# Row maxima of an attention taken over key tiles instead of from separate scores, in a one-core decoder layer

## The chip, the cores and the metric

The kernel runs on one core of a Trainium2 chip. The metric is the time of one execution on the device in microseconds; lower is better. TensorE (PE) multiplies matrices from SBUF into PSUM, VectorE (DVE), ScalarE (ACT) and GpSimd (POOL) do the elementwise work, SyncE (SP) issues most of the DMAs. PSUM has eight banks of 512 f32 for each of 128 partitions.

## The reference

One decoder layer on x [8, 512, 512] (f32) with a context [8, 512, 1024] and a mask over 512 positions of each of 8 batches. Three parts, each followed by a residual and a layer norm: a self-attention whose softmax runs over the 8 entries of the first axis (16 heads of 32), a cross attention (8 heads of 64), and a feed forward (512 to 2048 to 512) with a quantised hidden layer. The change touches the cross attention only:

```python
src_trans = (src @ W_src.T + b_src) * mask[:, :, None]      # [8, 512, 1024]: keys, values
tgt_trans = (tgt @ W_tgt.T + b_tgt) * mask[:, :, None]      # [8, 512, 512]: queries
scores = einsum('bthd,bshd->bhts', q, k) / sqrt(64)
scores = where(mask[:, None, None, :] == 0, -inf, scores)
attn = softmax(scores, axis=-1)
tgt_update = einsum('bhts,bshd->bthd', attn, v)
out = concatenate([tgt, tgt_update], axis=2) @ W_out.T + b_out
```

## The kernel before

The program has two halves, phase_a and phase_b (L955). phase_a does the self-attention and projects the context, and leaves the normed rows, the keys (already turned) and the values in HBM scratch, each as a high and a low f16 part. phase_b, in which the change lies, goes over the 8 batches. Every f32 product is made of three f16 products, high x high, low x high and high x low (terms, L47).

For each batch phase_b makes queries (queries, L1215; queries_masked, queries_hi and queries_low split them), then for 8 heads the attention, then the output projection (output_x1 for the half that needs no attention, output_rest for the other), a layer norm, and the turn of the normed rows into x2T (x2_transposes). The feed forward of a batch runs one turn of the loop later: while the heads of batch b+1 are worked, feed_forward1 (16 tiles of 12 matmuls, 128x512 out, into b_ff) and feed_forward2 (4 tiles of 16) of batch b fill TensorE between the steps of a head. In the heads of batch 0 there is no such work; there weight_transposes(n), n from 0 to 15, takes its place: four transposes of a w1 tile and four of a w2 tile into the two b_ff banks. It waits until ScalarE has copied the w2 tile of job n-1 (w2_done) and until VectorE has made the low part of the w1 tile of job n-1 (w1_lo).

A head's attention needs, for each query, the negated maximum of its scores as a row added by the product, since the scores that are used lie with keys on partitions (b_st) and the exponential's bias is a column over keys:

- scores(b, h, half), L1227: two matmuls each, queries on partitions, keys (512) along the bank, into b_sx0 and b_sx1;
- maximum, L1569: VectorE adds the mask row mneg and takes the maximum over 512 keys, for each of four tiles of 128 queries, into mxb; then L1580 writes the negated column into mz;
- maximum_row, L1235: four matmuls turn the column into a row of b_mr, and ScalarE copies that row into row 64 of q2 (L1408);
- transposed_scores(b, h, half), L1242: for each of four tiles of 128 keys two matmuls into b_st0 or b_st1, k1 x q1 (high and low keys with high queries) and k2 x q2 (high keys with low queries, and the row of maxima);
- exponentials, exponentials_high on ScalarE, exponentials_low on VectorE: exp into f32, then a high and a low f16 part, two key tiles at a time (p_hi, p_lo: 128x1024);
- values, L1253: 48 matmuls of 65 or 64 columns into b_av; normalized on VectorE divides by the sum.

The order in each engine's queue is written out by hand in heads (TensorE L1312, ScalarE L1462, VectorE L1612), and waits are semaphore counts. The maxima of head h+1 are found while head h is worked: TensorE's order in head h is scores(h+1, first half), transposed_scores(h, first half), values(h-1), scores(h+1, second half), feed_forward1(2h+1), transposed_scores(h, second half), maximum_row(h+1), feed_forward1(2h+2). The first head's scores come in queries_and_first_scores (L1357), amid the last tile of queries, and VectorE's side of it is queries_and_first_maximum (L1634). PSUM: two banks b_st, two b_sx, two b_ff, b_av and b_mr; at a batch's end the same banks serve for queries (tq_b) and for the output projection (om_b).

## Time and profile before

| | us |
|---|---|
| median of 3 runs | 1929.81 |
| lowest, highest | 1927.22, 1932.05 |
| the profiled execution | 1929.76 |
| its span, first to last instruction | 1927.9 |

| engine | busy us | share of the span |
|---|---|---|
| TensorE, matmuls | 1829.5 | 95% |
| TensorE, weight loads | 1003.3 | 52% |
| VectorE | 1333.2 | 69% |
| ScalarE | 785.3 | 41% |
| GpSimd | 558.7 | 29% |

phase_b takes from about 820 us to the end. Its batch 0 lies from about 835 to 935 us; each of the seven turns of the loop behind it takes about 129 us. In the rows L12 is line 12 of the kernel; PE is TensorE's matmuls, PEld its weight loads. A row's time is the start in us from the span's first instruction, and then the duration; matmuls overlap, so the distance between starts is what one costs in a row of them, and the duration is from its start to its last result. An idle time in brackets names what ended it.

### The profile page before, as it was taken

The page shows a single profiled execution, that of the slowest core. Times are in us where ns is not written, and L with a number is a line of the kernel's source. Part 1 is how long each engine was busy: PE and PEld are TensorE (multiplying, and loading weights), DVE is VectorE, ACT ScalarE, POOL GpSimd, SP SyncE. Part 2 cuts the span into 40 slices and gives each one's busy share as a digit, 9 for nine tenths or more (in the row PEclk, how much of TensorE's full clock was granted, in tenths as well). Part 3 has the DMA queues.
Part 4 walks back from the last instruction along what each step waited for, and adds up shares of the span by engine and source line. Part 5 has one row for each costly group of instructions (what it writes and reads, how often), then busy time and mean ns, then how long its engine had stood idle before and what let it go on. Part 6 is the DMA issues. An engine that isn't in the chain of part 4 may idle for free. (4 is left out here: it accounts for less than half of the span.)

```text
span 1927.9 us, 33302 instructions
## 1 busy us (share of the span) xinstructions
PE 1829.5 (95%) x12476; PEld 1003.3 (52%) x12476; DVE 1333.2 (69%) x1676; ACT 785.3 (41%) x1208; POOL 558.7 (29%) x576
## 2 busy tenths in 40 slices
PE   7999999999999989878899999999999999999998
PEld 3665465546554646445455454455454554554543
DVE  2899998999899998667465554655655646556521
ACT  3423222222222222248365363562653635626522
POOL 3135964786368345400102002003011020030010
PEclk9999999999999999979999999999999999999999
DMA  8436355425633566574413406207135052071010
GB/s 212 124 79 151 78 152 143 116 77 151 150 94 99 125 172 137 150 167 157 99 39 61 122 1 116 66 1 138 44 51 131 1 111 72 1 133 27 12 33 22
DMA packets 322654, 183.97 MB, mean 95 GB/s; under 512 B 225584, under 2 KB 278832, under 8 KB 322511
## 3 DMA queue, kind: packets, MB, share of 16 engines
q1 hardware_dynamic: 316448, 178.37, 38.9%
q10 hardware_dynamic: 6062, 3.49, 0.8%
q8 instruction: 114, 1.87, 0.4%
q14 instruction: 30, 0.24, 0.0%
HBM read 94.75 MB, written 33.55 MB: 67 GB/s over the span
## 5 line engine op out<-in xcount | busy, mean ns | idle before, releaser
L1531 DVE TENSOR_TENSOR p_lo<-k,p_hi 128x1024 f16<-128x1024 f32 x128 | 156.8, 1225 | 194.4 <-ACT p_hi L1404 194.4
L1176 POOL TENSOR_TENSOR q<-q,x_hi 128x512 f16<-128x512 f32 x28 | 37.6, 1374 | 638.7 <-ACT x_hi L1457 638.7
L1576 DVE CUSTOM_DVE_ANT_0 junk<-b_sx,mneg 128x512 f16<-128x512 f32 x256 | 175.9, 687 | 32.6 <-issue 23.2
L1204 PE MATMUL b_ff<-x2T_hi,w1T_hi 128*128 128x512 f16 x512 | 194.7, 380 | 1.9 <-DVE x2T_lo L1531 1.9
L1204 PE MATMUL b_ff<-x2T_lo,w1T_hi 128*128 128x512 f16 x512 | 194.7, 380 | 0.0
L1204 PE MATMUL b_ff<-x2T_hi,w1T_lo 128*128 128x512 f16 x512 | 194.6, 380 | 0.0
L1436 ACT ACTIVATE k<-b_st,mbias 128x512 f32<-128x512 f32 x256 | 161.9, 685 | 14.0 <-PE b_st L1250 13.4
L577 PE MATMUL sm_b<-cT_hi,wsT_hi 128*128 128x256 f16 x512 | 141.8, 277 | 15.2 <-DMA cT_lo<-rows_lo 13.6
L784 DVE TENSOR_TENSOR prod<-q,k 128x4096 f32<-128x4096 f32 x32 | 142.2, 4443 | 17.5 <-ACT q L660 16.7
L1404 ACT ACTIVATE p_hi<-k 128x1024 f16<-128x1024 f32 x128 | 135.3, 1057 | 45.5 <-PE b_av L1265 43.1
L1428 ACT ACTIVATE hq<-b_ff,b 128x512 fp8e4<-128x512 f32 x128 | 88.0, 687 | 155.6 <-PE b_ff L1204 149.0
L543 PE MATMUL pj_b<-winT_hi,xT_hi 128*128 128x512 f16 x384 | 146.8, 382 | 0.9 <-DVE winT_lo L851 0.9
L543 PE MATMUL pj_b<-winT_lo,xT_hi 128*128 128x512 f16 x384 | 146.8, 382 | 0.0
L543 PE MATMUL pj_b<-winT_hi,xT_lo 128*128 128x512 f16 x384 | 146.5, 382 | 0.0
L824 DVE TENSOR_TENSOR prod<-pr,v 128x4096 f32<-128x4096 f32 x32 | 142.4, 4451 | 1.1
L577 PE MATMUL sm_b<-cT_hi,wsT_lo 128*128 128x256 f16 x512 | 141.7, 277 | 0.0
L577 PE MATMUL sm_b<-cT_lo,wsT_hi 128*128 128x256 f16 x512 | 141.7, 277 | 0.0
L789 DVE TENSOR_REDUCE pr<-prod 128x128 f32<-128x4096 f32 x32 | 141.1, 4410 | 0.1
L1413 ACT ACTIVATE q<-q,rstdb 128x512 f32<-128x512 f32 x64 | 52.2, 815 | 216.4 <-POOL rstdb L88 216.3
L440 POOL TENSOR_TENSOR rows_lo<-cn,rows_hi 128x512 f16<-128x512 f32 x64 | 117.0, 1835 | 61.0 <-ACT rows_hi L644 60.9
L1204 PE MATMUL b_ff<-w2T,hq 128*128 128x512 fp8e4 x512 | 112.9, 379 | 1.6 <-ACT hq L1428 1.0
L82 POOL TENSOR_TENSOR vsb<-mvb,consts 128x1 f32<-128x1 f32 x64 | 14.9, 233 | 337.6 <-DVE mvb L1546 337.6
(272 smaller groups left out, 4368.9 us busy)
## 6 DMA issues: line engine op xcount, KB each, us to landing
cn<-in_ctx_dram SPq DMA_DIRECT2D x64, 256.0 KB, 3.1
k<-kT_scratch SPq DMA_DIRECT2D x24, 512.0 KB, 7.7
x<-in_x_dram SPq DMA_DIRECT2D x32, 256.0 KB, 3.1
x_scratch<-x SPq DMA_DIRECT2D x32, 256.0 KB, 2.2
q<-x_scratch SPq DMA_DIRECT2D x8, 1024.0 KB, 5.6
q<-x_scratch SPq DMA_DIRECT2D x32, 256.0 KB, 2.9
out_dram<-q SPq DMA_DIRECT2D x32, 256.0 KB, 4.4
xn<-in_x_dram SPq DMA_DIRECT2D x24, 256.0 KB, 2.9
```

Of the source, the lines that this page charges most:

```text
L440: pool.tensor_tensor(lo[:, :], row_source(kind, i), hi[:, :], ALU.subtract).then_inc(s["row_lo"], 1)
L543: pe.matmul(out, a, c, start=(j == 0 and m == 0), stop=False)
L577: pe.matmul(dst, a, z, start=(j == 0 and m == 0), stop=False)
L784: dve.tensor_tensor(prod[:, :, :], q[:, t, :].unsqueeze(1).to_broadcast([P, T, E]), k[:, :, :], ALU.mult).then_inc(s["sc_prod"], 1)
L789: dve.tensor_reduce(pr[:, t].rearrange("p h s -> p s h"), prod[:, :, :].rearrange("p s (h d) -> p s h d", h=H1), AX.X, ALU.add).then_inc(s ...
L824: dve.tensor_tensor(by_head(prod), probs, by_head(v), ALU.mult).then_inc(s["av_prod"], 1)
L1204: mm = pe.matmul(out, a, c, start=(start and n == 0), stop=end)
L1404: act.activation(dst, src, ACT.Copy, scale=scale).then_inc(done, 1)
L1428: act.activation(hq[:, f, :], ff_b[f % 2][:, :], ACT.Relu, bias=b1[:, f:f + 1], scale=1.0 / WS, saturate=False).then_inc(s["relu"], 1)
L1436: act.activation(pf[:, st, :], st_b[st % 2][:, :], ACT.Exp, bias=mbias[:, st:st + 1], scale=D2 ** -0.5).then_inc(s["st_exp"], 1)
L1531: dve.tensor_tensor(dst, bank, hi, ALU.subtract).then_inc(out, 1)
L1576: dve.tensor_tensor_reduce(junk[:, :], sx_b[tt % 2][:, :], mneg[:, :], 1.0, NEG, ALU.add, ALU.max, mx[:, h % 2, tt:tt + 1]).then_inc(s["sx ...
```

## The change

The scores with queries on partitions, their two banks and the mask row mneg are gone. b_st has four banks. For each head first_scores makes k1 x q1 into the four banks and leaves the sums open. On VectorE tops adds a mask column (0 or -60000) to each of the four banks in turn and keeps the larger of it and what top holds, element by element, so that top (128x512, f16) holds for each of 128 key positions and each query the maximum over the four key tiles. turned_tops turns top into b_mr by four matmuls with minus the identity, one tensor_reduce (negated_maxima) takes the minimum over 128 columns into mz, and maximum_row is as before. second_scores then adds k2 x q2 to the four open banks. The maximum is that of the first products alone; the softmax doesn't depend on the exact number subtracted.

The order is new on three engines. feed_forward1 can be issued in parts (i to j of its 12 matmuls); the first scores of head h+1 lie between parts of feed_forward1(2h+2), each behind the exponential that empties its bank; the turn lies before feed_forward1(2h+3), and maximum_row in it. For batch 0 a part that doesn't begin at 0 is nothing, and a part that does is the whole weight_transposes. The diff, cut to its core:

```diff
-    st_b = [bank(f"b_st{i}") for i in range(2)]
-    sx_b = [bank(f"b_sx{i}") for i in range(2)]
+    st_b = [bank(f"b_st{i}") for i in range(4)]
...
-    tq_b, om_b = [*st_b, mr_b, av_b], [*sx_b, *ff_b]
+    tq_b, om_b = [*st_b[0:2], mr_b, av_b], [*st_b[2:4], *ff_b]
...
-            def scores(b, h, half):
...
+            def first_scores(b, h, st):
+                if h:
+                    pe.wait_ge(s["st_exp"], 32 * b + 4 * (h - 1) + st + 1)
+                pe.matmul(st_b[st][:, :], k1[:, h, st * P:(st + 1) * P], q1[:, h, :], start=True,
+                          stop=True).then_inc(s["first_filled"], 1)
+
+            def turned_tops(b, h):
+                pe.wait_ge(s["topped"], 32 * b + 4 * h + 4)
+                for tt in range(4):
+                    mm = pe.matmul(mr_b[:, tt * P:(tt + 1) * P], top[:, tt * P:(tt + 1) * P], minus16[:, :],
+                                   start=True, stop=True)
+                mm.then_inc(s["mr_filled"], 1)
...
-            def transposed_scores(b, h, half):
...
+            def second_scores(b, h):
+                pe.wait_ge(s["mr_copied"], 8 * b + h + 1)
+                for st in range(4):
+                    pe.matmul(st_b[st][:, :], k2[:, h, st * P:(st + 1) * P], q2[:, h, :], start=False,
+                              stop=True, skip_group_check=True).then_inc(s["st_filled"], 1)
...
-            def feed_forward1(b, f):
+            def feed_forward1(b, f, i=0, j=12):
                 if b is None:
-                    return weight_transposes(f)
+                    return weight_transposes(f) if i == 0 else None
...
             def output_x1(ff):
+                if ff is None:
+                    pe.wait_ge(s["st_exp"], 32)
...
             def heads(b, ff):        # TensorE
                 feed_forward1(ff, 0)
                 pe.wait_ge(s["q_masked"], 4 * b + 4)
+                turned_tops(b, 0)
+                feed_forward1(ff, 1, 0, 6)
                 maximum_row(b, 0)
+                feed_forward1(ff, 1, 6, 12)
                 for h in range(H2):
+                    second_scores(b, h)
+                    if h + 1 == H2:
+                        values(b, h - 1)
+                        continue
+                    f = 2 * h + 2
...
-                    if h + 1 < H2:
-                        scores(b, h + 1, 0)
-                    transposed_scores(b, h, 0)
+                    feed_forward1(ff, f, 0, 2)
+                    first_scores(b, h + 1, 0)
+                    feed_forward1(ff, f, 2, 4)
+                    first_scores(b, h + 1, 1)
                     if h == 1:
                         pe.wait_ge(s["v_ld"], 80 * (b + 1))
                     if h:
                         values(b, h - 1)
-                    if h + 1 < H2:
-                        scores(b, h + 1, 1)
-                    feed_forward1(ff, 2 * h + 1)
-                    transposed_scores(b, h, 1)
-                    if h + 1 < H2:
-                        maximum_row(b, h + 1)
-                        feed_forward1(ff, 2 * h + 2)
+                    first_scores(b, h + 1, 2)
+                    feed_forward1(ff, f, 4, 6)
+                    first_scores(b, h + 1, 3)
+                    feed_forward1(ff, f, 6, 12)
+                    turned_tops(b, h + 1)
+                    feed_forward1(ff, f + 1, 0, 5)
+                    maximum_row(b, h + 1)
+                    feed_forward1(ff, f + 1, 5, 12)
...
             def queries_and_first_scores(b, ff):
-                scores(b, 0, 0)
+                first_scores(b, 0, 0)
+                first_scores(b, 0, 1)
                 queries(b, 3, slice(8, None))
-                scores(b, 0, 1)
+                first_scores(b, 0, 2)
+                first_scores(b, 0, 3)
...
             def heads(b, ff, rows=True):        # ScalarE
                 for h in range(H2):
+                    if h + 1 == H2:
+                        relu(ff, 2 * h + 1)
                     exponentials(b, h, 0)
+                    if h + 1 < H2:
+                        relu(ff, 2 * h + 1)
+                    exponentials(b, h, 1)
                     exponentials_high(b, h, 0)
-                    relu(ff, 2 * h + 1)
-                    exponentials(b, h, 1)
-                    if h + 1 < H2:
-                        maximum_row(b, h + 1)
                     exponentials_high(b, h, 1)
                     if h + 1 < H2:
                         relu(ff, 2 * h + 2)
+                        maximum_row(b, h + 1)
...
-            def maximum(b, h, half):
...
+            def tops(b, h, half):
+                for st in (2 * half, 2 * half + 1):
+                    n = 32 * b + 4 * h + st
+                    dve.wait_ge(s["first_filled"], n + 1)
+                    if st == 0:
+                        dve.tensor_scalar(top[:, :], st_b[0][:, :], mleast[:, 0:1], None, ALU.add).then_inc(
+                            s["topped"], 1)
+                    else:
+                        dve.wait_ge(s["topped"], n)
+                        stand_alone(dve, alone["dve"])
+                        dve.scalar_tensor_tensor(out=top[:, :], in0=st_b[st][:, :], scalar=mleast[:, st:st + 1],
+                                                 in1=top[:, :], op0=ALU.add, op1=ALU.max).then_inc(s["topped"], 1)
+
+            def negated_maxima(b, h):
+                dve.wait_ge(s["mr_filled"], 16 * b + 2 * h + 1)
+                dve.tensor_reduce(mz[:, 4 * (h % 2):4 * (h % 2) + 4, D2],
+                                  mr_b[:, :].rearrange("p (t c) -> p t c", t=4), AX.X, ALU.min).then_inc(s["negm"], 1)
...
             def heads(b, ff):        # VectorE
                 w1_low(ff, 0)
+                negated_maxima(b, 0)
+                w1_low(ff, 1)
                 for h in range(H2):
                     if h + 1 < H2:
-                        maximum(b, h + 1, 0)
+                        tops(b, h + 1, 0)
+                        tops(b, h + 1, 1)
+                    exponentials_low(b, h, 0)
+                    if h + 1 < H2:
+                        w1_low(ff, 2 * h + 2)
+                        negated_maxima(b, h + 1)
                     if h:
                         normalized(b, h - 1)
-                    if h + 1 < H2:
-                        maximum(b, h + 1, 1)
-                    exponentials_low(b, h, 0)
-                    w1_low(ff, 2 * h + 1)
                     exponentials_low(b, h, 1)
                     if h + 1 < H2:
-                        w1_low(ff, 2 * h + 2)
+                        w1_low(ff, 2 * h + 3)
...
-                maximum(b, 0, 0)
                 queries_low(b, 2)
+                tops(b, 0, 0)
                 queries_masked(b, 3)
-                maximum(b, 0, 1)
                 queries_low(b, 3)
+                tops(b, 0, 1)
```

In batch 0, ScalarE's relu(None, f) is weights_high(f), two copies out of the b_ff banks, and w1_low is VectorE's low part of the same tile; for all other batches w1_low is nothing.

## Rows read from the trace of the kernel before

**Rows 1.** Stretches: busy us (x instructions) by engine, PEclk the granted clock, DMA.
```profile
851.00:856.00 5.00, 2.98 (x18) 1.28 (x15) 4.58 (x12) 2.88 (x5) 0.00 (x0) 0.90 0.24 59
861.00:866.00 5.00, 3.56 (x12) 2.04 (x13) 2.58 (x4) 2.21 (x3) 0.00 (x0) 0.58 0.80 209
876.00:916.00 40.00, 33.05 (x400) 22.25 (x398) 33.07 (x75) 35.27 (x55) 0.00 (x0) 1.00 0.35 109
1493.00:1622.00 129.00, 127.06 (x949) 65.02 (x948) 73.17 (x151) 66.72 (x97) 14.80 (x36) 1.00 0.31 67
```

**Rows 2.** Timeline, TensorE, heads of batch 5: start, us, engine, line.
```profile
1512.23 0.59 PE L1232 MATMUL b_sx<-k,q 128*128 128x512 f16 x2
...
1541.09 0.59 PE L1232 MATMUL b_sx<-k,q 128*128 128x512 f16 x2
...
1542.56 0.20 PE L1262 MATMUL b_av<-v_hi,p_hi 128*128 128x65 f16 x1
...
1544.02 0.59 PE L1232 MATMUL b_sx<-k,q 128*128 128x512 f16 x2
...
1547.04 0.38 PE L1249 MATMUL b_st<-q,k 128*128 128x512 f16 x1
...
1547.90 0.39 PE L1238 MATMUL b_mr<-ident,mz 128*65 128x128 f16 x4
1548.13 0.38 PE L1204 MATMUL b_ff<-x2T_hi,w1T_hi 128*128 128x512 f16 x1
```

**Rows 3.** Timeline, the same batch: handovers between the engines.
```profile
1550.89 1.23 DVE L1531 TENSOR_TENSOR p_lo<-k,p_hi 128x1024 f16<-128x1024 f32 x1 [3.20 <-ACT p_hi L1404]
...
1551.00 0.69 ACT L1428 ACTIVATE hq<-b_ff,b 128x512 fp8e4<-128x512 f32 x1
...
1552.18 0.20 PE L1262 MATMUL b_av<-v_hi,p_hi 128*128 128x65 f16 x1 [0.44 <-DVE p_lo L1531]
...
1557.34 7.07 PE L1204 MATMUL b_ff<-w2T,hq 128*128 128x512 fp8e4 x32
...
1564.44 0.69 DVE L1606 TENSOR_TENSOR f16o<-b_ff,b2q 128x512 f16<-128x512 f32 x1 [0.98 <-PE b_ff L1204]
```

**Rows 4.** VectorE: groups by line and form (busy us, mean ns), one timeline row.
```profile
L1576 DVE CUSTOM_DVE_ANT_0 junk<-b_sx,mneg 128x512 f16<-128x512 f32 x224 | 153.9, 687 | 26.5 <-issue 20.4 <-PE b_sx L1232 6.1
L1563 DVE SCALAR_TENSOR_TENSOR qf<-b_st,bt,mrow 128x512 f32<-128x512 f32 x14 | 10.5, 750 | 5.4 <-PE b_st L1204 4.9
...
L789 DVE TENSOR_REDUCE pr<-prod 128x128 f32<-128x4096 f32 x32 | 141.1, 4410 | 0.1
...
1596.91 0.18 DVE L1546 BATCH_NORM_AGGREGATE mvb<-statsb 128x2 f32<-128x6 f32 x1 [0.15 <-DVE statsb L1543]
```

**Rows 5.** Timeline, the start of batch 6's heads.
```profile
1607.25 1.28 DVE L1531 TENSOR_TENSOR x2T_lo<-b_ff,x2T_hi 128x512 f16<-128x512 f32 x2
...
1607.58 0.59 PE L1232 MATMUL b_sx<-k,q 128*128 128x512 f16 x2
...
1622.11 0.59 PE L1232 MATMUL b_sx<-k,q 128*128 128x512 f16 x2
```

**Rows 6.** Timeline, batch 0: heads 0, 2 and 7, ScalarE in head 6, output_x1.
```profile
854.51 0.39 PE L1249 MATMUL b_st<-q,k 128*128 128x512 f16 x1 [0.25 <-ACT q L1408]
...
875.29 0.38 PE L1249 MATMUL b_st<-q,k 128*128 128x512 f16 x1
...
905.61 0.59 ACT L1408 ACTIVATE q<-b_mr 1x512 f16<-1x512 f32 x1
906.23 1.06 ACT L1404 ACTIVATE p_hi<-k 128x1024 f16<-128x1024 f32 x1
...
908.28 1.27 ACT L1436 ACTIVATE k<-b_st,mbias 128x512 f32<-128x512 f32 x2
...
915.19 0.38 PE L1249 MATMUL b_st<-q,k 128*128 128x512 f16 x1
...
920.01 0.38 PE L1204 MATMUL b_sx<-wxT_hi,x1T_hi 128*128 128x512 f16 x1
```

58 lines of the change are left out of this document (18 added, 40 removed).

## The prediction

> **What bounds the kernel now.** I read the busy time by stage first, then TensorE's order of time in one head, then what VectorE and ScalarE hand to it. From batch 1 on TensorE is the bound: 127.06 of 129.00 us at a granted clock of 1.00, VectorE and ScalarE near half [rows 1]. A head takes (1541.09 - 1512.23) / 3 = 9.62 us [rows 2]. The 512-column matmuls start 3.02 / 14 = 0.216 us apart, the 48 of values() take 1.46, the four of maximum_row 0.23 (1547.90 to 1548.13) [rows 2]; 36 x 0.216 + 1.46 + 0.23 = 9.47 is work and 0.15 is waiting. A matmul ends 0.38 us after it starts [rows 2]. A wait that VectorE ends costs TensorE 0.06 (1552.12 to 1552.18), one that TensorE ends costs VectorE 0.03 (1564.41 to 1564.44) [rows 3]. In batch 0 the heads hold weight transposes in place of feed forward products; TensorE isn't full there, and VectorE and ScalarE set 7.98 us a head, (915.19 - 875.29) / 5 [rows 6].
>
> **What goes and what comes, in counts.** Each of 64 heads loses 4 of 36 matmuls (the scores with queries on partitions) and gains four of 128 columns. TensorE work per full head becomes 32 x 0.216 + 1.46 + 0.23 + 0.23 = 8.83, 0.64 less. If that were all, 56 heads would give 36 us. But the row of maxima now takes a longer way: four VectorE operations that hang on each other, a turn on TensorE, a reduction on VectorE, the old turn, the copy. And first_scores fill all four b_st banks, so each waits for an exponential of the head before.
>
> **New VectorE costs.** tops() is a scalar_tensor_tensor with a pointer scalar on a PSUM tile: its nearest row is L1563, 0.75 us; the removed reduction, 0.687, is the lower bound. Each waits for the one before with a stand_alone between, as BATCH_NORM_AGGREGATE does: 0.15; the lower bound is none [rows 4]. The first top has no second tensor; I put it at 0.75 too. tensor_reduce over 512: 1024 elements of p_lo take 1.23 and 512 of L1576 take 0.687 [rows 3, 4], so 1.06 ns an element and 0.14 fixed, 0.68; an eighth of the 4.41 for 4096 elements, 0.55, is the lower bound [rows 4]. The row shows 0.75 for 512 f32 elements from PSUM with a pointer scalar. The Trainium skill (VectorE: DVE Perf Modes, the section on the TRN2 errata) gives 120 cycles plus one per element for a PSUM source, at 0.96 GHz an estimate of 0.66 us for each top; L1563 disagrees, and by the page a full head would be about 0.2 us shorter.
>
> **A full head, T = its second_scores.** TensorE: 4 seconds to 0.86, 2 products, first 0 at 1.29, 2 products, first 1 at 1.94, values(h-1) 2.16 to 3.62, first 2 at 3.62, 2 products, first 3 at 4.26, 6 products to 5.77. ScalarE: the first two exponentials 0.41 to 1.68, relu to 2.27, the other two to 3.44 (1.27 a pair [rows 6], relu 0.69 [rows 3], 0.1 of overlap), so no bank is waited for. VectorE: top 2 at 3.62 + 0.38 + 0.03 = 4.03 to 4.78, top 3 4.93 to 5.68; the turn starts at 5.77, just unhindered. Then exponentials_low, 1.23, stands ahead of the reduction in VectorE's queue: it ends at 6.83 and the reduction at 7.43 (0.08 of overlap each). TensorE has done the turn and 5 products at 7.07 and waits for the reduction until 7.49: 0.42 us. Behind that waiting matmul stand the remaining 7 products and the next head's second scores. 7.49 + 0.23 + 1.51 = 9.22. The copy of the row ends at 8.5, hidden by the 7 products; normalized and the second exponentials_low end near 9.2 and are needed by values at 11.4. So a full head gains 0.40, not 0.64. With both lower bounds (0.69, 0.05 gaps) it is 9.0; with 0.1 more per new operation 9.5.
>
> **The start of a batch.** Before, from the first scores at 1607.58 to head 1 at 1622.11 is 14.53 us [rows 5]. After: VectorE is free at 1607.25 + 1.28 = 1608.53 [rows 5]; queries_low(2) 0.69, tops 0 and 1 (1.65), queries_masked(3) 0.75 [rows 4], ScalarE's f16 copy 0.6 (between half of p_hi's 1.06 [rows 6] and relu's 0.69), queries_low(3) 0.69, tops 2 and 3 (1.65), less overlap: topped at 1614.30. TensorE is through feed_forward1(0) at 1611.9 and stands 2.4 us. Turn, 6 products, maximum row, 6 products: T0 = 1617.38. Head 0 has no values: first 2 waits 0.75 for its exponential and maximum_row 0.45 for the reduction, 8.68 in all. Head 7 has 0.86 + 1.46 = 2.32 before feed_forward2.
>
> **Sum of a full batch.** Before, to the start of feed_forward2: 14.53 + 5 x 9.62 + (1557.34 - 1541.09) = 78.9 [rows 2, 3, 5]. After: 9.80 + 8.68 + 6 x 9.22 + 2.32 = 76.1. The gain is 2.8; seven batches give -19 us. Per 0.1 us of a head's period this moves 4. Nothing behind feed_forward2(0) changes: its first sum comes 1.5 us later on VectorE, but values(7) stands ahead of the next user.
>
> **Batch 0.** Here what was put after what matters more. weights_high(2h+1) now stands behind the first two exponentials, its w1_low behind that, and weight_transposes(2h+2) waits for both, ahead of all first scores: everything is in one chain. From T: exponentials to 1.68, two copies to 2.66 (0.97 for two, 907.29 to 908.28 [rows 6]), transposes 2.71 to 3.58, first 0 and 1 to 4.01, values to 5.47, first 2, top 2 5.88 to 6.63, top 3 6.78 to 7.53, exponentials_low to 8.68, w1_low to 9.28, reduction to 9.88, maximum_row at 9.93, filled at 10.31, copy 0.59, T' = 10.98 (that includes p_hi 1.06 x 2 and two copies beside it, to 8.7). Before: 7.98. Five heads cost 15.0. Heads 0 and 1 took 20.8 with waits for weight loads [rows 6]; by the same steps 20.5 to 25, and I take 24.4. The first maximum row comes 1.8 later. At the end output_x1 comes 3.55 after the last T, before 920.01 - 915.19 = 4.82: -1.3. Sum +19 us at full clock. TensorE now stands 1.85, 1.7, 0.95 and 0.8 us in each of these heads, about half of it. In 851 to 856, busy 2.98 of 5.00 us, the granted clock fell to a mean of 0.90, and in 861 to 866, behind more stops, it was 0.58, while the denser heads of 876 to 916 kept 1.00 [rows 1]. At 1.2 GHz TensorE's pieces on the chain (the first seconds, transposes, first scores, values, turns) cost 3.6 us a head more. I take half of the time of the five heads at that level, as the mean of the two rows, 0.74, has it: +9. The bounds are 0 and 25 for all seven heads.
>
> **Total.** 1929.8 (the profiled execution, with the span of 1927.9; the median of the runs is the same) - 19 + 19 + 9 = 1939, +0.5%. A measurement of this kernel can tell 0.3%, 5.8 us, from no change.
>
> **Rivals.**
> 1. The forecast, both effects about as worked out: 1930 to 1952, around 1939; 0.45.
> 2. The clock stays at 1.00 in batch 0. For it: in 876 to 916 it did, with VectorE as the bound too. Against: 851 to 866, and the stops get longer. 1929.8 - 19 + 19 = 1930. The Trainium skill (TensorE: Matmul & The Clock Gate, HAM oscillation) says that a loop with long waits loses its clock in every turn; by that the clock part is nearer its upper bound, 1950. Chance of full clock 0.15.
> 3. VectorE's chain is short (tops 0.69, no gaps) or the queries at a batch's start hand over sooner: heads 9.0, batch -4.3, seven -30; batch 0 +17 with a clock part of 0 to 9: 1917 to 1926. It ends faster. The rows of the removed reduction speak for 0.69, those with a pointer scalar against. 0.20.
> 4. The turn misses its place: from top 3 ending over 0.05 us later (5.73 against 5.77) TensorE stops twice a head. At 0.15 us more per top the turn starts at 6.03, maximum_row at 7.79, the head takes 9.53 and a batch's start 0.6 more, so a full batch gains 0.3 at most: 1929.8 - 2 + 28 = 1956. 0.15.
> 5. The change doesn't do what it says: counts of matmuls are fixed by the code, so TensorE's busy share will fall; 0.05 for a load or wait elsewhere (the next batch's keys wait for the last p_lo) that adds some us: 1950.
>
> **Range and chances.** The low end takes most of rival 3, the high end most of 1 and 5 and some of 4: 1918 to 1954. Faster by over 0.3% (under 1924): 0.17. Within: the rest of 3, rival 2 and the low part of 1: 0.28. Slower (over 1935.6): 0.55.
>
> **What would show it.** In the trace after: 9.2 us from one head's second scores to the next in batches 1 to 7, with TensorE idle 0.4 us before maximum_row, released by the reduction; 2.4 us before the first turn of a batch, released by a top; batch 0 heads of 11 to 14 us with granted clocks under 1.00 between 860 and 935; tops of 0.75 us, a reduction of 0.68. If batch 0 grows by under 15 us, or full heads take under 9.0, I am wrong on the slow side; if the turn itself waits in every head, on the fast side.

## The result, and the profile after

The kernel after takes 1970.33 us (median; 1964.87 to 1976.07), the one before 1930.93 beside it: a ratio of 1.0207, 95% interval 1.0166 to 1.0248. It is 2% slower, where 1939 was forecast with 1954 as the high end of the range. The profiled execution took 1964.87, with a span of 1963.1; it is the fastest of the four, 5.5 us under the median. The account below is of that one; the slowest two, 1974.98 and 1976.07, had a mean granted clock of 0.964 against its 0.974.

The page of the kernel after, busy us (share of the span), the granted clock in 40 slices, and the groups of the new VectorE operations:

```profile
PE 1813.1 (92%) x12476; PEld 994.8 (51%) x12476; DVE 1377.5 (70%) x1421; ACT 769.5 (39%) x1208; POOL 561.4 (29%) x576
...
PEclk9999999999999999888999999999999999999999
...
L1598 DVE SCALAR_TENSOR_TENSOR top<-b_st,mleast,top 128x512 f16<-128x512 f32 x192 | 144.1, 750 | 57.7 <-PE b_st L1230 39.4
...
L1593 DVE TENSOR_SCALAR top<-b_st,mleast 128x512 f16<-128x512 f32 x64 | 48.0, 750 | 127.0 <-PE b_st L1230 127.0
```

TensorE is 16 us less busy than before, and still the span is 35 us longer: the work went down and waiting came in its place. To see where, I cut the span of each profiled execution at the first scores of each batch (line 1230 after, 1232 before; rows 5 has one of them). Batch 0 is the stretch from its first scores to those of batch 1, "1 to 6" that from those of batch 1 to those of batch 7. The columns behind them are parts of a full batch: **start** is from its first scores to head 0's second scores (**slow starts** counts those of batches 1 to 7 in which it took 11.3 to 11.4 us), **head** the mean from one head's second scores to the next's in heads 1 to 6, **jump** the mean over batches 1 to 6 from the first matmul of output_x1 to the first of output_rest, where TensorE's loop jumps back. In batch 7, where the loop is left and nothing jumps back, this last stretch takes 10.36 us in every trace. The runs of the section below are in the table too; how long a kernel's whole time is stands with each.

| kernel | first half | batch 0 | 1 to 6 | last | start, us | slow starts | head | jump, us |
|---|---|---|---|---|---|---|---|---|
| before | 848.2 | 113.2 | 775.6 | 191.0 | - | - | 9.62 | 10.66 |
| after | 852.3 | 145.3 | 777.1 | 188.4 | 9.69 or 11.38 | 4 | 9.36 | 11.80 |
| e9, after again | 846.7 | 149.6 | 782.6 | 188.6 | 9.72 or 11.39 | 5 | 9.36 | 12.09 |
| e1_fill | 846.8 | 141.7 | 765.0 | 189.3 | 9.71 | 0 | 9.36 | 10.88 |
| e2_tops_first | 846.3 | 148.9 | 759.6 | 187.7 | 7.88 | 0 | 9.36 | 11.80 |
| e3_weights_early | 845.3 | 136.5 | 777.5 | 190.0 | 9.71 or 11.39 | 5 | 9.36 | 11.84 |
| e4_reduce_first | 846.3 | 147.5 | 760.3 | 186.7 | 9.71 or 11.38 | 3 | 8.91 | 12.05 |
| e5_small_v | 843.4 | 142.2 | 768.3 | 190.1 | 9.71 or 11.38 | 4 | 9.36 | 10.60 |
| e6_keys_early | 849.8 | 140.6 | 768.5 | 191.5 | 9.71 or 11.39 | 4 | 9.36 | 10.63 |
| e7_late_transposes | 845.8 | 127.6 | 778.6 | 191.3 | 9.68 or 11.39 | 6 | 9.36 | 11.51 |
| e8_all4 | 848.4 | 121.2 | 733.8 | 184.9 | 7.88 | 0 | 8.91 | 10.56 |
| e10_before_keys | 849.0 | 113.2 | 775.6 | 192.1 | - | - | - | 10.69 |
| e11_all4_fill | 845.1 | 125.2 | 734.7 | 184.1 | 7.88 | 0 | 8.91 | 10.69 |
| e12_shift113 | 847.2 | 149.3 | 771.3 | 190.2 | 9.70 or 11.38 | 5 | 9.36 | 10.80 |
| e13_shift40 | 851.0 | 151.9 | 776.2 | 191.3 | 9.71 or 11.38 | 5 | 9.36 | 11.49 |

The first half isn't touched by any of these edits; its 843 to 852 us is what one execution differs from another, and the 4.1 us by which the two in the first lines differ say nothing of the change. Of the other 31 us between before and after, 32.1 lie in batch 0, +1.5 in batches 1 to 6, and the last gains 2.6.

Stretches of the kernel after; the columns are as in rows 1, the last three the granted clock, the DMA share (it can exceed 1, since packets' times overlap) and GB/s. The first three lie in batch 0, then come the starts of batches 1, 2 and 6, then batch 5:

```profile
860.00:880.00 20.00, 12.36 (x75) 7.51 (x75) 9.07 (x12) 10.84 (x18) 0.00 (x0) 0.68 0.92 301
880.00:900.00 20.00, 12.57 (x126) 8.14 (x123) 13.28 (x20) 10.52 (x16) 0.00 (x0) 0.83 0.24 73
900.00:920.00 20.00, 12.03 (x144) 8.30 (x141) 11.19 (x17) 12.03 (x19) 0.00 (x0) 0.91 0.29 92
...
1002.00:1007.00 5.00, 2.85 (x20) 1.55 (x20) 2.70 (x4) 1.28 (x2) 0.00 (x0) 1.00 0.50 120
1130.00:1135.00 5.00, 3.06 (x13) 1.41 (x14) 2.44 (x4) 0.56 (x1) 0.00 (x0) 0.72 0.54 131
1650.00:1655.00 5.00, 3.94 (x17) 2.05 (x18) 1.56 (x3) 0.37 (x1) 0.00 (x0) 0.66 0.66 158
1514.41:1644.39 129.98, 124.10 (x948) 63.53 (x949) 78.70 (x120) 65.01 (x96) 15.29 (x36) 0.99 0.32 68
```

Batch 0 has lost the clock of 1.00 that it had [rows 1]. A full batch now has TensorE idle for 5.9 of 130.0 us, against 1.9 of 129.0 [rows 1].

**A full head.** The timeline of one in batch 5, TensorE and then VectorE:

```profile
1543.83 1.03 PE L1251 MATMUL b_st<-q,k 128*128 128x512 f16 x4
...
1547.45 0.38 PE L1230 MATMUL b_st<-q,k 128*128 128x512 f16 x1
...
1549.39 0.38 PE L1203 MATMUL b_ff<-x2T_hi,w1T_lo 128*128 128x512 f16 x1
1549.70 0.40 PE L1237 MATMUL b_mr<-minus,top 128*128 128x128 f16 x4
...
1551.43 0.41 PE L1244 MATMUL b_mr<-ident,mz 128*65 128x128 f16 x4 [0.26 <-DVE mz L1603]
...
1553.19 0.38 PE L1251 MATMUL b_st<-q,k 128*128 128x512 f16 x1
```
```profile
1548.01 1.63 DVE L1598 SCALAR_TENSOR_TENSOR top<-b_st,mleast,top 128x512 f16<-128x512 f32 x2 [0.83 <-PE b_st L1230]
1549.56 1.22 DVE L1549 TENSOR_TENSOR p_lo<-k,p_hi 128x1024 f16<-128x1024 f32 x1
1550.69 0.69 DVE L1603 TENSOR_REDUCE mz<-b_mr 128x4 f16<-128x512 f32 x1
```

From 1543.83 to 1553.19 are 9.36 us. TensorE waits in the two places that were named: for the last top (1549.39 to 1549.70 are 0.31 us where matmuls start 0.216 apart), and for the reduction, which stands behind exponentials_low. The head before took 9.62 [rows 2].

**The start of a batch.** TensorE in batch 6; the [rows 5] of before lie in the same place:

```profile
1648.49 0.38 PE L1203 MATMUL b_ff<-x2T_hi,w1T_lo 128*128 128x512 f16 x1
1651.06 0.61 PE L1237 MATMUL b_mr<-minus,top 128*128 128x128 f16 x4 [2.19 <-DVE top L1598]
1651.46 0.63 PE L1203 MATMUL b_ff<-x2T_hi,w1T_hi 128*128 128x512 f16 x1
1651.88 0.63 PE L1203 MATMUL b_ff<-x2T_lo,w1T_hi 128*128 128x512 f16 x1
```

The wait for the tops came as forecast (matmul starts 2.57 us apart). What wasn't in the forecast is behind it: the 512-column matmuls start 0.42 us apart and not 0.22, which is TensorE at 1.2 GHz instead of 2.4. Of this comes 11.38 instead of 9.69 us. It happened in 4 of the 7 batches here and in 41 of the 63 of the nine rows of the table that have this wait. The wait is as long where the clock held (2.15 to 2.19 us of idle time in all 63), so its length alone doesn't decide between the two.

**The jump.** TensorE and SyncE (SPq are its DMA issues) in the loop turn that ends at 1751, of the kernel after, and then SyncE's in the same turn of the kernel before:

```profile
1750.00 0.38 PE L1203 MATMUL b_ff<-wxT_hi,x1T_lo 128*128 128x512 f16 x1
1751.91 0.39 PE L1203 MATMUL b_st<-wxT_hi,oT_hi 128*128 128x512 f16 x1 [1.53 <-issue]
...
1728.92 0.33 SPq L1054 DMA_DIRECT2D mrow<-in_mask_dram  x1
...
1732.47 8.56 SPq L1066 DMA_DIRECT2D v_hi<-v_scratch  x4
1741.13 0.79 SPq L1068 DMA_DIRECT2D v_lo<-v_scratch  x1
```
```profile
1690.16 0.33 SPq L1055 DMA_DIRECT2D mrow<-in_mask_dram  x1
...
1695.15 6.89 SPq L1067 DMA_DIRECT2D v_hi<-v_scratch  x4
1702.13 0.79 SPq L1069 DMA_DIRECT2D v_lo<-v_scratch  x1
```

TensorE stands 1.53 us for nothing that a semaphore tells ("issue"). In this turn feed_forward2 begins at 1722.84 after and 1686.47 before. SyncE's loads of the next batch start when the last exponentials_low of this one is done: 6.1 us behind that mark after, 3.7 before. So the last load of values is issued at +18.3 instead of +15.7 us, and all that SyncE issues behind it moves along.

**A head of batch 0**, TensorE in head 2 of the kernel after (before: [rows 6]):

```profile
876.23 1.09 PE L1196 MATMUL b_ff<-ident,x2T_hi 128*128 128x128 f32 x4 [1.78 <-ACT w2T L1436]
...
877.97 1.06 PE L1230 MATMUL b_st<-q,k 128*128 128x512 f16 x2
880.61 0.60 PE L1230 MATMUL b_st<-q,k 128*128 128x512 f16 x2
...
882.87 0.40 PE L1237 MATMUL b_mr<-minus,top 128*128 128x128 f16 x4 [1.66 <-DVE top L1598]
```

The chain is the one that was worked out: exponentials, weight copies, transposes, first scores, tops, turn. The eight transposes take 1.74 us (876.23 to 877.97), at 1.2 GHz; in e1_fill, at a granted clock of 1.00, they take 0.90 (885.11 to 886.01), where 0.87 was forecast.

### The profile page after: what moved, and what is told of

Same layout as the page of the kernel before. It is cut to its first block and busy times, and to the rows that moved or that the text cites. A ratio compares the mean times of both kernels' runs of the same rounds, so it can differ in the third digit from the quotient of the medians.

```text
span 1963.1 us, 32964 instructions
## 1 busy us (share of the span) xinstructions
PE 1813.1 (92%) x12476; PEld 994.8 (51%) x12476; DVE 1377.5 (70%) x1421; ACT 769.5 (39%) x1208; POOL 561.4 (29%) x576
## 3 DMA queue, kind: packets, MB, share of 16 engines
q10 hardware_dynamic: 6062, 3.49, 0.8%
## 5 line engine op out<-in xcount | busy, mean ns | idle before, releaser
L1549 DVE TENSOR_TENSOR p_lo<-k,p_hi 128x1024 f16<-128x1024 f32 x128 | 162.2, 1268 | 33.9 <-ACT p_hi L1420 33.9
L1598 DVE SCALAR_TENSOR_TENSOR top<-b_st,mleast,top 128x512 f16<-128x512 f32 x192 | 144.1, 750 | 57.7 <-PE b_st L1230 39.4
L785 DVE TENSOR_TENSOR prod<-q,k 128x4096 f32<-128x4096 f32 x32 | 142.1, 4440 | 19.1 <-ACT q L661 18.3
L578 PE MATMUL sm_b<-cT_lo,wsT_hi 128*128 128x256 f16 x512 | 142.2, 278 | 0.0
L1420 ACT ACTIVATE p_hi<-k 128x1024 f16<-128x1024 f32 x128 | 128.6, 1057 | 32.4 <-PE b_av L1266 32.4
L1593 DVE TENSOR_SCALAR top<-b_st,mleast 128x512 f16<-128x512 f32 x64 | 48.0, 750 | 127.0 <-PE b_st L1230 127.0
```

The lines of the kernel that those rows point to most:

```text
L578: pe.matmul(dst, a, z, start=(j == 0 and m == 0), stop=False)
L785: dve.tensor_tensor(prod[:, :, :], q[:, t, :].unsqueeze(1).to_broadcast([P, T, E]), k[:, :, :], ALU.mult).then_inc(s["sc_prod"], 1)
L1420: act.activation(dst, src, ACT.Copy, scale=scale).then_inc(done, 1)
L1549: dve.tensor_tensor(dst, bank, hi, ALU.subtract).then_inc(out, 1)
L1598: dve.scalar_tensor_tensor(out=top[:, :], in0=st_b[st][:, :], scalar=mleast[:, st:st + 1], in1=top[:, :], op0=ALU.add, op1=ALU.max).then_i ...
```

## The experiments

e1 to e4 ran on one chip, e5 to e8, e9 to e11 and e12 with e13 on one other each, always beside the kernel before. Its medians there, 1930.8 to 1933.1, are alike, so the times are compared across the groups too.

**e1_fill.** Idle matmuls in TensorE's waits, 8 at the start of a full batch and 15 in each head of batch 0.

```diff
+            def fill(h, n):
+                for _ in range(n):
+                    pe.matmul(mr_b[:, :], k1[:, h, 0:P], q1[:, h, :], start=True, stop=True)
...
+                fill(0, 8 if ff is not None else 0)
                 turned_tops(b, 0)
...
                     f = 2 * h + 2
+                    fill(h, 8 if ff is None else 0)
...
+                    fill(h, 7 if ff is None else 0)
                     turned_tops(b, h + 1)
```

> The changed kernel with matmuls into b_mr that nobody reads, put where TensorE stands: 8 of 512 columns ahead of the first turn of a batch in batches 1 to 7, and 8 behind second_scores and 7 ahead of the turn in each head of batch 0. They are shorter than the stops (2.4 us; 1.85 and 1.7 us), so they can only act through the clock. Theory A, the stops let the granted clock fall and that costs time: first scores to T0 is 9.7 us in all batches (now 11.4 in four of seven), the heads of batch 0 go from 12.5 us in the mean to 11.0 at a clock of 1.00, the whole is 15 to 19 us shorter than the changed kernel, near 1953. Rival B, the clock only falls where TensorE has nothing to do anyway and the chain through VectorE and ScalarE sets the time: no stretch changes by over 0.3 us, 1965 to 1975 stays.

1944.21 us, ratio 1.0059 (1.0034 to 1.0085). The start of batch 6, and a stretch of batch 0:

```profile
1630.34 1.89 PE L1317 MATMUL b_mr<-q,k 128*128 128x512 f16 x8
1632.69 0.40 PE L1237 MATMUL b_mr<-minus,top 128*128 128x128 f16 x4 [0.46 <-DVE top L1605]
1632.93 0.38 PE L1203 MATMUL b_ff<-x2T_hi,w1T_hi 128*128 128x512 f16 x1
...
880.00:900.00 20.00, 17.46 (x181) 10.80 (x182) 12.91 (x20) 11.55 (x19) 0.00 (x0) 1.00 0.35 105
```

More work and less time: 26 us under the median of the kernel after, where 15 to 19 were expected; 5.5 to 7 of it lie in the jumps, which the idle matmuls weren't put there for (see e12). All seven starts take 9.6 to 9.7 us, so the slow ones are the clock's alone. In batch 0, from head 2 on, the clock is 1.00 and five heads take 11.27 to 11.30 us each, 56.4 in all, where before has 7.98 each and after 11.29 to 13.32: the order costs 3.3 us a head, the clock up to 2.0 more. The two heads of batch 0 that have a granted clock of 1.00 in the kernel after take 11.29 as well. In heads 0 and 1 the clock stayed at 0.89 and 0.80 in spite of the idle matmuls, and they take 13.25 and 13.71. The idle matmuls don't shorten the chain, from head 2 on they only keep its pieces on TensorE fast.

**e2_tops_first.** At a batch's start the four tops stand ahead of the masking of the fourth query tile and of its low part, and the turn no longer waits for that tile (head 1 does).

```diff
-                pe.wait_ge(s["q_masked"], 4 * b + 4)
+                pe.wait_ge(s["q_masked"], 4 * b + 3)
                 turned_tops(b, 0)
...
                 tops(b, 0, 0)
-                queries_masked(b, 3)
-                queries_low(b, 3)
                 tops(b, 0, 1)
+                queries_masked(b, 3)
+                if ff is None:
+                    queries_low(b, 3)
...
                 negated_maxima(b, 0)
+                if ff is not None:
+                    queries_low(b, 3)
```

> The changed kernel; at the start of a batch all four tops come ahead of queries_masked(3) on VectorE, and queries_low(3) behind the first reduction. Theory A, the wait ahead of the first turn is VectorE's queue and its length lets the clock fall: topped comes 2.0 us earlier, first scores to T0 is 8.1 to 8.4 us in every batch instead of 9.7 or 11.4, 16 to 20 us less in the whole, near 1952. If the wait were set by the first scores themselves or by the reduction: T0 moves by under 0.5 us and the four long starts stay.

1949.65 us, ratio 1.0086 (1.0057 to 1.0114). All seven starts take 7.88 us, 1.8 less than a start at full clock and 3.5 less than a slow one; the wait is 0.33 to 0.36 us and the clock never falls there:

```profile
1633.62 0.40 PE L1237 MATMUL b_mr<-minus,top 128*128 128x128 f16 x4 [0.36 <-DVE top L1599]
```

Batches 1 to 6 take 759.6 us against 777.1 and 782.6 in the two profiled executions of the kernel after.

**e3_weights_early.** In batch 0 ScalarE copies the weights of job 2h+1 ahead of the first two exponentials.

```diff
-                    if h + 1 == H2:
+                    if h + 1 == H2 or ff is None:
                         relu(ff, 2 * h + 1)
                     exponentials(b, h, 0)
-                    if h + 1 < H2:
+                    if h + 1 < H2 and ff is not None:
                         relu(ff, 2 * h + 1)
```

> The changed kernel; in batch 0 alone ScalarE's weights_high(2h+1) is put back ahead of the first two exponentials of head h. Theory A, weights_high, w1_low, weight_transposes, first scores, tops, reduction are one chain: transposes start 1.6 us earlier after second_scores, a head takes 10.9 us in the mean instead of 12.5 (9.4 where the clock is full), batch 0 is 10 to 12 us shorter, near 1960. Rival C, batch 0 is set by VectorE's sum of work and the weight loads: under 3 us less.

1954.86 us, ratio 1.0114 (1.0069 to 1.0159). Batch 0 takes 136.5 us, 9 to 13 less than after; its heads go from 11.3 to 13.3 us to 10.3 to 13.1, 11.6 in the mean and not the 10.9 expected; the granted clock was under 1.00 in all of them (0.50 to 0.85).

**e4_reduce_first.** In full heads the reduction stands ahead of the first exponentials_low.

```diff
                         tops(b, h + 1, 1)
+                    if h + 1 < H2 and ff is not None:
+                        negated_maxima(b, h + 1)
                     exponentials_low(b, h, 0)
-                    if h + 1 < H2:
+                    if h + 1 < H2 and ff is None:
                         w1_low(ff, 2 * h + 2)
                         negated_maxima(b, h + 1)
```

> The changed kernel; in batches 1 to 7 VectorE does negated_maxima(h+1) ahead of exponentials_low(h, first half) instead of behind it. Theory A, the 0.4 us that TensorE stands ahead of the row of maxima is exponentials_low in VectorE's queue: a full head takes 9.0 us instead of 9.36, 6 heads in 7 batches give 15 to 17 us, near 1954. Rival D, the later exponentials_low then holds up values or the next exponentials: heads stay at 9.3 or get longer, with TensorE waiting for p_lo.

1945.65 us, ratio 1.0068 (1.0042 to 1.0094). A head in batch 5, VectorE and TensorE, and then one of its jumps:

```profile
1526.52 0.70 DVE L1603 TENSOR_REDUCE mz<-b_mr 128x4 f16<-128x512 f32 x1 [0.49 <-PE b_mr L1237]
1527.12 1.22 DVE L1549 TENSOR_TENSOR p_lo<-k,p_hi 128x1024 f16<-128x1024 f32 x1
...
1527.39 0.39 PE L1244 MATMUL b_mr<-ident,mz 128*65 128x128 f16 x4
...
1473.18 0.38 PE L1203 MATMUL b_ff<-wxT_hi,x1T_lo 128*128 128x512 f16 x1
1476.17 0.39 PE L1203 MATMUL b_st<-wxT_hi,oT_hi 128*128 128x512 f16 x1 [2.61 <-issue]
...
1477.02 0.63 PE L1203 MATMUL b_st<-wxT_hi,oT_hi 128*128 128x512 f16 x1
1477.45 0.63 PE L1203 MATMUL b_st<-wxT_lo,oT_hi 128*128 128x512 f16 x1
```

A head takes 8.91 us, 0.08 over the 8.83 of its work on TensorE: maximum_row waits no more. The 0.45 us less in each of 7 heads are 3.2 us in each of seven batches, 22 in all, where 15 to 17 were expected from 0.36 us in each of 6 heads. The longest jump of all (2.99 us between starts) shows that a stop there can take the clock as well: behind it matmuls start 0.43 us apart.

**e5_small_v** and **e6_keys_early** take two causes from the jump. In e5 the loads of v in the loop move 4 partitions instead of 128, so it leaves out most of v from batch 1 on and its output is wrong; in e6 the loads of mask and keys wait for the exponentials.

```diff
+                rows = slice(0, P if first else 4)
...
-                    sp.dma_start(v_hi[:, st, :, 0:D2], v_in[b, 0][:, st, :].rearrange("p (h d) -> p h d", h=H2)
+                    sp.dma_start(v_hi[rows, st, :, 0:D2], v_in[b, 0][rows, st, :].rearrange("p (h d) -> p h d", h=H2)
```
```diff
                 if not first:
-                    sp.wait_ge(s["p_lo"], 16 * b)
+                    sp.wait_ge(s["st_exp"], 32 * b)
```

> The kernel after, but with the loads of v inside the loop cut from 128 partitions to 4, so most of v is left out from batch 1 on; nothing else is changed. Place looked at: from output_x1 to output_rest on TensorE, where the loop jumps back. It takes 10.5 to 10.8 us before and 11.1 to 12.5 after, and the difference is idle time that no semaphore ends, 0.6 to 1.9 us. Theory A (since the last exponentials_low of a batch comes 2.4 us later against feed_forward2, SyncE starts the keys and values later, and the DMA queues are still full of them when TensorE's next instructions are fetched at the jump): the stretch takes 10.4 to 10.8 in each of batches 1 to 6, about 1.1 us less a batch, the total 6 to 8 us less than the kernel after, some 1960. Theory B (the stop has to do with the program's size or with where the jump stands in memory, not with what the DMA engines move): 11.1 to 12.5 as before, total unchanged near 1968.

> The kernel after, with one wait changed: SyncE's loads of the next batch's mask and keys wait for the batch's last exponentials (their last reader is done then) and not for the last exponentials_low. The keys are then issued near the start of feed_forward2 instead of 6.1 us behind it, the values 1.5 to 2 us earlier than after. Theory A (the loads' place against the jump costs the time): output_x1 to output_rest takes 10.5 to 11.0 us, 0.8 to 1.2 less a batch, total 5 to 7 us less than after, some 1962. Theory B (it isn't the loads, or the values alone count and 1.6 us is too little): 11.1 to 12.5 stays, total near 1968.

1953.97 us, ratio 1.0113 (1.0083 to 1.0144), and 1954.09, ratio 1.0095 (1.0059 to 1.0132). The jump takes 10.60 and 10.63 us, 10.36 to 10.80 in single batches, so theory A holds in both. TensorE's program is the same in the three kernels. The 3 us ahead of the stop in after and in e6, with e6's stop:

```profile
1747.00:1750.00 3.00, 3.00 (x15) 1.34 (x14) 0.00 (x0) 0.00 (x0) 0.00 (x0) 1.00 2.05 113
```
```profile
1476.24:1479.24 3.00, 3.00 (x16) 1.35 (x14) 0.00 (x0) 0.00 (x0) 0.00 (x0) 1.00 0.61 95
...
1479.24 0.38 PE L1203 MATMUL b_ff<-wxT_hi,x1T_lo 128*128 128x512 f16 x1
1479.89 0.39 PE L1203 MATMUL b_st<-wxT_hi,oT_hi 128*128 128x512 f16 x1 [0.27 <-issue]
```

Between kernels the DMA share in the 3 us ahead of the stop goes with its length: 0.42 to 0.97 with 0.21 to 0.90 us between starts where the loads are early or small (before, e5, e6, e8, e10, e11), 0.65 to 2.22 with 0.83 to 2.99 where they are late and the loop isn't moved (after, e2, e3, e4, e7, e9). Stop by stop it doesn't: ahead of the longest, e4's, it was 0.81. e6's last load of values is issued at +14.0 us, 4 us earlier and not 1.5 to 2. The total fell by 15 us against e9_after_again, not by the 5 to 8 expected. The table, whose profiled executions are 23.5 and 17.0 us under e9's, shows the rest: the jumps gave 9 us over six batches, and two slow starts fewer another 3.4; batch 0 gave 7 to 9, of which 3.0 and 3.5 lie behind output_rest, since the turned rows of batch 1 come in time there; the rest is the clock in its heads. TensorE waits 3.49 us for the rows after, 0.16 in e6, and 1.91 before:

```profile
983.32 0.59 PE L1203 MATMUL b_st<-x1T_hi,wtT_hi 128*128 128x512 f16 x1 [3.49 <-DMA x1T_lo<-q]
```
```profile
978.88 0.38 PE L1203 MATMUL b_st<-x1T_hi,wtT_hi 128*128 128x512 f16 x1 [0.16 <-DMA x1T_lo<-q]
```
```profile
949.91 0.38 PE L1204 MATMUL b_st<-x1T_hi,wtT_hi 128*128 128x512 f16 x1 [1.91 <-DMA x1T_lo<-q]
```

**e7_late_transposes.** In batch 0 no first scores wait for a weight: the transposes stand behind them and behind maximum_row, and e3's edit is in.

```diff
-                    feed_forward1(ff, f, 0, 2)
+                    if ff is not None:
+                        feed_forward1(ff, f, 0, 2)
...
-                    feed_forward1(ff, f, 6, 12)
+                    feed_forward1(ff, f, 6 if ff is not None else 0, 12)
                     turned_tops(b, h + 1)
-                    feed_forward1(ff, f + 1, 0, 5)
+                    if ff is not None:
+                        feed_forward1(ff, f + 1, 0, 5)
                     maximum_row(b, h + 1)
-                    feed_forward1(ff, f + 1, 5, 12)
+                    feed_forward1(ff, f + 1, 5 if ff is not None else 0, 12)
```

> The kernel after, changed in batch 0 alone: the transposes of weights 2h+2 stand behind the four first scores and ahead of the turn of the tops, those of 2h+3 behind maximum_row, and ScalarE's copies of weights 2h+1 ahead of the first exponentials. Nothing of a head's chain then waits for a weight. Theory A (batch 0's loss is the one chain from exponentials over weight copies and transposes to first scores): a head takes 9 to 10.5 us instead of 11.3 to 13.3, from the first scores of batch 0 to those of batch 1 about 125 us (145.3 after, 136.5 with the copies early alone), total some 18 us less than after, near 1950. Theory B (it is the new work on VectorE and the turn itself, or the clock, that makes the heads long): 11 us or more a head, over 136 for the batch, total not under 1956.

1945.21 us, ratio 1.0062 (1.0044 to 1.008). Heads take 9.1 to 10.7 us, batch 0 127.6, 18 to 22 less than after, as theory A has it (batch 0 2.6 over its figure). So the larger part of the loss in batch 0 was the one chain over the weights. Not all: 14.4 us against before are left, 2.9 of them ahead of head 0's second scores, 8.2 in the heads (the tops, the turn, and a granted clock of 0.81 to 1.00) and 3.4 behind output_rest.

**e8_all4.** e2, e6 and e7 together, and the reduction first in every head, batch 0's too.

> The four edits together: tops of head 0 ahead of the masks and low parts of the fourth query tile, the reduction ahead of exponentials_low in every head, batch 0 as in the run before this one, keys early. If the causes add up: first scores to second scores 7.9 us in every full batch (clock stays at 1.00, since no wait of over 1 us is left), heads 8.9, output_x1 to output_rest 10.5 to 11, a full batch 122.5 us against 129.3 before and 129.3 on average after; batch 0 120 to 126 against 113.2 before. Total 1933 - 7 x 6.7 + 10 = about 1896, faster than the kernel before by 1.5 to 2.3%. Rival (the granted clock still falls in batch 0 and the stop at the jump stays): batch 0 133, 123.5 a full batch, 1912.

1886.14 us (1885.94 to 1890.13), ratio 0.9758 (0.9735 to 0.978): 2.4% faster than the kernel before, 4.2% faster than the changed one (1969.11 in the run after this). The page, and batch 5:

```profile
PE 1788.9 (95%) x12476; PEld 992.9 (53%) x12476; DVE 1381.2 (73%) x1421; ACT 769.6 (41%) x1208; POOL 561.4 (30%) x576
...
1459.16:1581.27 122.11, 121.05 (x948) 63.49 (x949) 79.34 (x120) 64.79 (x96) 15.22 (x36) 1.00 0.32 72
```

The same instructions on TensorE as in the kernel after, and 1.1 us idle in a full batch. The causes add up: in the stages of the table e8 stands to before with +8.0 us in batch 0, -41.8 in batches 1 to 6 and -6.1 in the last. Against the kernel after the starts give 17.6 us in batches 1 to 6, the heads 18.9 and the jumps 7.4, in all 43.9, and 43.3 were measured. The median is 10 us under the forecast of 1896; batch 0 was 2 us cheaper, the profiled execution took 1890.1, and the rest isn't broken down.

**e9_after_again.** The kernel after, unchanged, on the chip of e10 and e11.

> The kernel after, unchanged, on the chip of the experiments. Its four runs so far gave 1965 to 1976, with the granted clock at 0.964 to 0.974; the kernels that leave its full batches as they are but for one small edit gave 1954. Theory A (the time hangs on how many of the seven 2.4 us waits let the clock fall, on batch 0's clock and on the stops at the jump, all of which differ from run to run): a median of 1958 to 1968, a spread of 10 us or more, and in the profiled run each full batch either 127.7 or less where the clock held in the wait or 129 to 130.5 where it fell. Theory B (the kernel is steady and the chip made the difference): all runs within 4 us of one another.

1969.11 us, all five runs within 1966.83 to 1970.81, ratio 1.0192 (1.0179 to 1.0205). The spread is theory B's, 4 us, but the median is that of the first four runs, so the chip doesn't explain the difference to the small edits either; that is in the stages, as said under e6. Neither theory holds whole. What each batch took is the sum of its start and its jump, as in theory A, but only three of six lie within A's figures: the one whose clock held took 128.88 us for its long jump, one with a slow start 130.63, and one 132.98, where a long jump (12.98) took the clock as well. Batch 0's clock between 860 and 940 us was 0.68 in this execution and 0.81 in the first:

```profile
860.00:940.00 80.00, 54.31 (x428) 36.40 (x428) 44.83 (x63) 38.72 (x62) 0.00 (x0) 0.68 0.32 108
```
```profile
860.00:940.00 80.00, 49.03 (x438) 31.58 (x438) 46.19 (x65) 44.69 (x72) 0.00 (x0) 0.81 0.39 123
```

**e10_before_keys.** e6's edit in the kernel before.

> The kernel before, with the one wait of SyncE changed that e6_keys_early changes in the kernel after. Theory A (the gain of e8_all4 over the kernel before comes from the new order of the maxima, the early keys only take back a loss of it): output_x1 to output_rest goes from 10.55 to 10.8 down to 10.4 at the best, total 1 to 2 us less than before, ratio 0.999 to 1.000. Rival (the early loads are worth much by themselves): over 8 us less, ratio under 0.996.

1930.03 us, ratio 0.9992 (0.998 to 1.0003), jump 10.69 and no shorter. The early keys are worth nothing, within the interval, where the loads weren't late; so e8's gain over the kernel before is that of the new order.

**e11_all4_fill.** e8 with six idle matmuls in each head of batch 0 ahead of the turn.

```diff
+                    fill(h, 6 if ff is None else 0)
                     turned_tops(b, h + 1)
```

> e8_all4 with six more 512-column matmuls in each head of batch 0 ahead of the turn of the tops, into a bank that the turn overwrites; they lie in TensorE's wait for the tops. Theory A (part of batch 0's heads is still lost to the clock, granted 0.83 to 1.00 there): heads of 9.4 us in all of batch 0, T7 - T0 66 instead of 68.5, the total 2 to 4 us less, 1883. Theory B (VectorE, busy 7.8 of 9.5 us, is what holds the heads and the clock costs nothing there): T7 - T0 68 to 70, total 1886 or up to 4 more, since the extra matmuls can stand in the way.

1892.84 us, ratio 0.9802 (0.9788 to 0.9815), 6.7 more than e8; heads of batch 0 take 9.7 to 10.9 us instead of 9.4 to 10.4, and T7 - T0 is 71.8, over the figures of both theories. Theory A's premise stands: in e8 the heads at a granted clock of 1.00 take 9.4 us and those at 0.84 take 10.1. But the idle matmuls don't hold the clock here (four of seven heads at 0.82 to 0.87), and heads at 0.99 to 1.00 take 9.7 to 9.9: they stand in the way and win nothing back.

**e12_shift113, e13_shift40.** e1 has the loads as late as after (values' last at +18.0 us), and short jumps nevertheless, 10.88. Its loop stands further on in TensorE's program. These two move that place alone.

```diff
+                for _ in range(113 if ff is None else 0):
+                    pe.matmul(mr_b[:, 0:64], k1[:, 0, 0:P], q1[:, 0, 0:64], start=True, stop=True)
                 turned_tops(b, 0)
```

> The kernel after, with 113 idle matmuls of 64 columns (113 weight loads with them) in batch 0, ahead of the first turn of tops, into a bank that the turn overwrites. Nothing in the loop is changed, but TensorE's loop stands 226 instructions later in its program, about as far as in e1_fill, whose stops at the jump were short (10.88 us on average from output_x1 to output_rest) though its loads were as late as in the kernel after (11.8). Theory A (the stop hangs on what the DMA queues move at the jump, and also on where the jump and its target stand in the program): 10.6 to 11.1 us in batches 1 to 6. Theory B (the place in the program doesn't matter, e1_fill was short for another reason, such as its even clock): 11.5 to 12.5. Batch 0 is some 4 us longer in both cases.

> The same with 40 idle matmuls, 80 instructions. Theory A: a value of its own between 10.5 and 12.5 us, which with that of 113 idle matmuls and that of the kernel after (11.8 and 12.1 in two profiled runs) differs by more than the 0.3 between these two. Theory B: 11.5 to 12.5 in both.

1957.57 us (1.0137, 1.0102 to 1.0173) and 1966.63 (1.0184, 1.0109 to 1.0259), two runs of each; e13's are 11.7 us apart. The jumps take 10.80 us (10.55 to 11.01) and 11.49 (11.32 to 11.83), against 11.80 and 12.09 in the unshifted kernel. e12's loads are as late as after (+18.1 to +18.5), and the unshifted kernels with late loads (after, e9, e2, e3, e4, e7) all lie from 11.51 to 12.09, so e12 and e1 speak for theory A. e13 doesn't: e7 has 11.51 without a shift. Both things count, then: how late the loads are against the jump, and, by e12 and e1, where the loop lies in the program. The Trainium skill (Runtime: NRT & Kernel Launch, Instruction fetch mechanics) says that a taken branch to a page that isn't held makes the engine wait for a DMA of that page; that fits both findings, but no trace here shows the fetch itself. How the place acts isn't settled by one distance that shows an effect.

## Why the prediction was wrong, point by point

**Full heads** (forecast 9.22, measured 9.36). The mechanism was right: VectorE's tops, 0.75 us each, and 0.42 us of waiting before maximum_row because the reduction stands behind exponentials_low. The term that was mis-sized is the handover to the last pair of tops. I had top 2 start 0.41 us behind the start of its first scores; it starts 0.56 behind (1547.45 to 1548.01): the stand_alone that was counted between two tops stands ahead of every top but the first in the program, also of one that has waited for TensorE. Top 0, which has none, starts 0.42 us behind its scores. So the turn slips 0.1 behind its place (the point at which rival 4 begins) and the reduction with it. 0.14 x 6 heads x 7 batches = 5.9 us.

**The start of a batch** (forecast 9.80, measured 9.69). Right, with its 2.4 us wait. But the wait's second price was left out. In batch 0 I had counted waits against the clock, from rows 1; the same rows speak for a loss here too, and I didn't apply them outside batch 0. Four slow starts cost 1.7 us each, 6.7 in the profiled execution, a term that the sum has at nothing; e1_fill and e2_tops_first show it by its absence. The rule that I cited from the Trainium skill (TensorE: Matmul & The Clock Gate, HAM oscillation), that a loop with long waits loses its clock in every turn, was weighed for batch 0 alone. It bears on this wait too, but wouldn't have given its price: the clock was lost in 41 of 63 turns and not in every one, behind waits shorter than those of the page's example.

**"Nothing behind feed_forward2(0) changes"** is the step that failed outright. SyncE's queue stands behind the last exponentials_low, 2.4 us later than before; I had followed TensorE's and VectorE's queues there, and only named the wait as a rival worth 0.05. The jumps cost 70.8 - 64.0 = 6.8 us in batches 1 to 6, and the same late loads cost 4.4 us at the end of batch 0, 29.1 instead of 24.7 from output_rest on (the queries of batch 1 wait for turned rows, and the clock falls behind that wait). e5 and e6 show the cause, e4 and e9 that it can reach the clock.

**Batch 0's heads** (forecast +26.3 from head 0's second scores to output_x1, measured 91.1 - 65.5 = +25.6). The mechanism was right, and the sum too, but by some luck: at full clock a head was put at 10.98 and e1 shows 11.28, 1.5 us too little for the five heads; for the clock in them I had +9, and 62.1 - 56.4 = 5.7 us were measured, 3.3 too much. Heads 0 and 1 took 25.5 us and not 24.4. e9, at 0.68, lost 7 us more in its heads, which lies in the bounds that were given.

**The sum.** 1929.8 + 4.1 (first half) + 32.1 (batch 0; +28 forecast) + 1.5 - 2.6 (full batches; -19.6 forecast) = 1964.9. Of the 18.5 us that the full batches came out worse, heads are 5.9, slow starts 6.7, jumps 6.8, and the starts themselves give 0.8 back. Batch 0 is 4.1 over its forecast, by the late loads at its end. The first half's 4.1 us are chance.

**The rivals.** Rival 2, a full clock in batch 0, is excluded by the granted clock of 0.68 to 0.91 there; rival 3, a short chain, by 0.75 us a top. The turn slipped past its place by 0.1 us, a little of rival 4. Rival 5's mechanism, late keys, was real, and cost the 11 us that it was given (6.8 + 4.4); it came on top of everything else, where I had it as one case in twenty.

## What to carry to other kernels

Count a new wait on TensorE twice: its length, and what the work behind it costs at half the clock, in every turn of a loop and not only where the trace of before shows a low clock. When the last user of a buffer moves later, follow the DMA queue that waits for it to the end of the loop: the loads that it issues may meet the next instructions' own. And when work is taken off a full engine, the chain that replaces it has to be put first in each queue that it crosses: here four moves, three in those queues and one in SyncE's, turn a loss of 2% into a gain of 2.4%.

## What the runs showed of the hardware that was not expected

- A TensorE wait of 2.2 us (2.6 from one matmul's start to the next) in a loop that is otherwise full took the clock to 1.2 GHz for some 8 matmuls (1.7 us lost) in 41 of 63 cases, and waits of the same length didn't in the other 22; eight idle matmuls in it held the clock in 7 of 7, and six or fifteen in each head of batch 0 held it in some heads and not in others (e11, e1).
- Where the loop jumps back TensorE stood between 0.2 and 3.0 us from one matmul to the next, longer where the next batch's loads are late; 226 more instructions ahead of the loop shortened it by 0.9 to 1.3 us in the mean, in one trace each of two kernels (e12, e1).
- With a column from SBUF as scalar a VectorE operation on 512 f32 elements of PSUM takes 0.75 us, the same with one tensor operand (line 1593) and with two (line 1598); with a constant as scalar scalar_tensor_tensor takes 0.69 (line 1553, 16 of them in batch 0).
